# Two attention layers with feed-forwards: adding the turned maxima to the queries on TensorE and ScalarE instead of VectorE

## The reference, cut to what matters

```python
f = log_sigmoid(x @ Wf.T + bf)              # per head
c = cumsum(f, axis=1)
scores = einsum('bihd,bjhd->bhij', q, k) / sqrt(8)
scores = scores + (c[:, :, None, :] - c[:, None, :, :]).transpose(0, 3, 1, 2)
scores = where(tril, scores, -inf)
p = softmax(scores, axis=-1)
o = einsum('bhij,bjhd->bihd', p, v)
```

## Time and profile before

| | before |
|---|---|
| median of 3 runs | 1479.36 us (1478.53 to 1481.83) |
| the profiled execution, its own time | 1476.44 us |
| span of its instructions | 1474.2 us |
| busy over the span: PE, DVE, ACT, POOL | 75%, 78%, 62%, 31% |
| loop of the second attention | about 815 to 1267 us of the span |
| granted TensorE clock, mean of the span | 0.812 |

### The profile page before, as it was taken

The page is one execution under the profiler, slowest core; times in us unless marked ns, Lnnn a source line. Parts: engine busy times, 40 slices in busy tenths (PEclk is TensorE's granted clock), DMA queues, the critical chain, the costliest instruction groups (busy, mean ns, idle before and its releaser), DMA issues. The chain is left out here.

```text
span 1474.2 us, 26809 instructions
## 1 busy us (share of the span) xinstructions
PE 1103.8 (75%) x7861; PEld 517.4 (35%) x7861; DVE 1143.3 (78%) x3615; ACT 910.5 (62%) x1823; POOL 460.4 (31%) x680
## 2 busy tenths in 40 slices
PE   1556666666542799995377899999999999677995
PEld 0112222222232466663254233233233332243654
DVE  4699999999988544443867899999999998377664
ACT  1699999999962244332464566666666666356453
POOL 0132333233220677775102122222222222122331
PEclk9755555555555899998598799999999999799998
DMA  1356867786638222222626111111111111400001
GB/s 57 96 124 139 152 129 139 140 147 133 117 68 235 65 80 76 78 80 96 216 97 191 59 57 53 66 54 56 63 54 59 56 54 37 115 1 1 1 15 44
DMA packets 221078, 128.95 MB, mean 87 GB/s; under 512 B 164632, under 2 KB 200600, under 8 KB 220552
## 3 DMA queue, kind: packets, MB, share of 16 engines
q1 hardware_dynamic: 200312, 100.90, 28.0%
q0 software_dynamic: 6896, 16.04, 3.4%
q10 hardware_dynamic: 13728, 10.30, 2.6%
HBM read 55.60 MB, written 37.62 MB: 63 GB/s over the span
## 5 line engine op out<-in xcount | busy, mean ns | idle before, releaser
L1863 ACT ACTIVATE qkv_made<-qkv_lower 128x1024 f32<-128x1024 f32 (+3 forms) x256 | 208.0, 872 | 105.8 <-PE qkv_lower L1679 105.8
L522 PE MATMUL a_sc<-a_k,a_q 16*128 16x512 bf16 (+3 forms) x384 | 165.4, 504 | 124.2 <-DVE a_mx L701 117.9
L1643 PE MATMUL qkv_upper<-l_k,all_y 64*128 64x512 bf16 (+3 forms) x768 | 211.8, 338 | 44.8 <-DVE qkv_mx L2057 25.3
L2053 DVE CUSTOM_DVE_ANT_0 all_y<-qkv_upper,all_mask 128x384 bf16<-128x384 f32 (+3 forms) x512 | 231.5, 485 | 9.2 <-PE qkv_upper L1643 3.0
L1909 POOL TENSOR_SCALAR_AFFINE_SELECT qkv_made<-qkv_made 128x256 f32<-128x256 f32 x256 | 102.5, 406 | 364.8 <-ACT qkv_made L1863 274.9
L701 DVE CUSTOM_DVE_ANT_0 a_rows<-a_sc,all_mask 128x1024 bf16<-128x1024 f32 (+7 forms) x256 | 191.4, 748 | 8.0 <-PE a_sc L522 7.4
L571 ACT ACTIVATE a_rows<-a_rows 128x1024 bf16<-128x1024 bf16 (+7 forms) x256 | 171.5, 670 | 24.5 <-DVE a_rows L711 24.5
L1679 PE MATMUL qkv_lower<-all_y,l_k 64*128 64x384 bf16 (+3 forms) x768 | 173.5, 330 | 6.6 <-DVE all_y L2074 0.9
L2057 DVE TENSOR_REDUCE qkv_mx<-qkv_upper 128x1 f32<-128x512 f32 x256 | 173.1, 687 | 6.8 <-PE qkv_upper L1643 6.8
L1698 PE MATMUL qkv_upper<-qkv_made,qkv_v_heads 128*32 128x384 f32 (+3 forms) x1920 | 177.5, 433 | 0.0
L580 ACT ACTIVATE a_unread<-a_rows 128x1024 bf16<-128x1024 bf16 (+7 forms) x256 | 171.1, 668 | 0.0
(11 more groups left out here) (258 smaller groups left out, 1897.1 us busy)
## 6 DMA issues: line engine op xcount, KB each, us to landing
qkv_made<-out_rows SPq DMA_DIRECT2D x16, 512.0 KB, 8.0
o_rows<-qkv_made SPq DMA_DIRECT2D x32, 256.0 KB, 2.0
l_k<-k_rows SPq DMA_DIRECT2D x60, 128.0 KB
all_y<-q_rows SPq DMA_DIRECT2D x128, 48.0 KB
a_raw<-in_gate ACTq DMA_DIRECT2D x16, 224.0 KB, 3.2
a_raw<-in_up ACTq DMA_DIRECT2D x16, 224.0 KB, 4.1
ride_wd<-in_down SPq DMA_DIRECT2D x1, 3584.0 KB, 16.9
k_rows<-qkv_parts SPq DMA_DIRECT2D x8, 384.0 KB, 3.3
```

The source lines that it names most:

```text
L522: last = nc.tensor.matmul(sc[:, n % 3, lo // 512, 0:w], q_sb[32 * h:32 * h + hd, u % 2, qb * P:(qb + 1) * P], k_sb[32 * h:32 * h + hd, u % ...
L1643: nc.tensor.matmul(row[:, n % SLOTS, 0:w], q_sb[of_head, u % RING, POS[qb] * P:(POS[qb] + 1) * P], k_sb[of_head, u % RING, lo:lo + w], sta ...
L1863: nc.scalar.activation(probs[:, n % GR, lo:hi], st[:, n % 2, lo:hi], ACT.Exp).then_inc(exp_done, 1)
L2053: nc.vector.tensor_tensor_reduce(out=passed[:, n % SLOTS, 0:w], in0=tile[:, 0:w], in1=mask[:, at:at + w], scale=1.0, scalar=-3e38, op0=ALU ...
```

## The change

The turn becomes two entries, a first and a second half. For each half TensorE writes 512 float32 columns (one slot of `row`): a matmul of the identity with the unit's queries, which puts the queries there, and on top of it, accumulating, the four transposes of the blocks of maxima. ScalarE copies the slot to `q_sb` in bfloat16. VectorE's addition is gone. The halves stand between two pieces in slots 7 and 8, and the pieces behind them are spread so that each of the 12 slots has two pieces. The slots of PSUM held by halves are freed by a new semaphore `turn_copied`, those held by pieces by `row_free`, whose count now leaves the halves out. ScalarE copies the halves of unit u + 1 after the exponentials of groups 8 and 9 of unit u, and those of unit 0 ahead of its first exponentials. The list of semaphores of the expert stage is taken in another order.

```diff
-TURN = "turn"
+TURNS = ("turn first half", "turn second half")
...
 LATER = ((12, 13), (14, 15), (16, 17), (18, 19), (20, 21), (22, 23),
-         (0, 1), (2, 3), (TURN,), (4, 5, 6), (7, 8, 9), (10, 11))
+         (0, 1), (2, TURNS[0], 3), (4, TURNS[1], 5), (6, 7), (8, 9), (10, 11))
...
+            def slot_free(n):
+
+                if n >= SLOTS:
+                    before = entries[n - SLOTS]
+                    if before in turn_of:
+                        pe.wait_ge(turn_copied, turn_of[before] + 1)
+                    else:
+                        pe.wait_ge(row_free, maxed_of[before] + 1)
...
-                if n >= SLOTS:
-                    pe.wait_ge(row_free, n - SLOTS + 1)
+                slot_free(n)
...
-            def turn_max(u):
-
-                n = entry_of[u, TURN]
+            def turn_max(u, what):
+
+                half, n = TURNS.index(what), entry_of[u, what]
                 pe.wait_ge(m_parts, 3 * (u + 1))
-                pe.wait_ge(row_free, n - SLOTS + 1)
-                turned = row[:, n % SLOTS].bitcast(BF16)
-                for qb in range(TB):
-                    last = nc.tensor.transpose(turned[:, POS[qb] * P:(POS[qb] + 1) * P],
-                                               mcol[:, u % 2, qb].rearrange("p h r -> p (h r)"), ident_b[:])
+                slot_free(n)
+                tile = row[:, n % SLOTS]
+                nc.tensor.matmul(tile[:], ident_b[:], q_sb[:, u % RING, 512 * half:512 * (half + 1)], start=True, stop=False,
+                                 skip_group_check=True)
+                for to in range(4):
+                    last = nc.tensor.matmul(tile[:, to * P:(to + 1) * P],
+                                            mcol[:, u % 2, ORDER[4 * half + to]].rearrange("p h r -> p (h r)"), ident_b[:],
+                                            start=False, stop=True, skip_group_check=True)
                 last.then_inc(row_ready, 1)
...
                     if g == 0:
 
-                        pe.wait_ge(row_free, entry_of[u, TURN] + 1)
+                        pe.wait_ge(turn_copied, 2 * (u + 1))
...
             for u, what in opening[NC // 2:]:
                 entry(u, what)
-                if what == TURN:
+                if what == TURNS[1]:
                     pe.wait_ge(remains, len(todo))
...
+            def copy_turned(u, half):
+
+                e = (u, TURNS[half])
+                act.wait_ge(row_ready, entry_of[e] + 1)
+                nc.scalar.copy(q_sb[:, u % RING, 512 * half:512 * (half + 1)], row[:, entry_of[e] % SLOTS]
+                               ).then_inc(turn_copied, 1)
+
+            copy_turned(0, 0)
+            copy_turned(0, 1)
             for u in range(units):
...
                     if g == 0 and u:
                         copy_out(u - 1)
+                    if g in (8, 9) and u + 1 < units:
+                        copy_turned(u + 1, g - 8)
             copy_out(units - 1)
...
-            def add_max(u):
-                n = entry_of[u, TURN]
-                dve.wait_ge(row_ready, n + 1)
-                nc.vector.tensor_tensor(out=q_sb[:, u % RING], in0=row[:, n % SLOTS].bitcast(BF16),
-                                        in1=q_sb[:, u % RING], op=ALU.add).then_inc(row_free, 1)
```

More of the change, by code:

```diff
@@ L409, with of_next @@
 LATER = ((12, 13), (14, 15), (16, 17), (18, 19), (20, 21), (22, 23),
-         (0, 1), (2, 3), (TURN,), (4, 5, 6), (7, 8, 9), (10, 11))
+         (0, 1), (2, TURNS[0], 3), (4, TURNS[1], 5), (6, 7), (8, 9), (10, 11))
+def of_next(what):
+    return what in TURNS or what >= NC // 2
 def row_entries(units):
@@ L420, in row_entries @@
             for what in slot:
-                to = u + 1 if what == TURN or what >= NC // 2 else u + 2
+                to = u + 1 if of_next(what) else u + 2
                 if to < units:
@@ L1071, in experts @@
         at, pos, cnt = ht[:, 0], dn[:, 0], dn[:, 1]
+        scattered = [c.sem(f"scattered{j}") for j in range(OUT)]
         listing = ("tables", "chain", "ex_ready", "ones_set", "ranked", "marked",
@@ L1080, in experts @@
          made_ready) = (c.sem(n) for n in names)
-        scattered = [c.sem(f"scattered{j}") for j in range(OUT)]
         block = ctx.enter_context(nc.Block())
@@ L1416, in project_and_attend @@
     entry_of = {e: i for i, e in enumerate(entries)}
+    turn_of = {e: i for i, e in enumerate(e for e in entries if e[1] in TURNS)}
+    maxed_of = {e: i for i, e in enumerate(e for e in entries if e[1] not in TURNS)}
     with ExitStack() as ctx:
@@ L1460, in project_and_attend @@
         of_y, of_x = Spread(nc, c, "y"), Spread(nc, c, "x")
[L1461 to L1464, removed]
+        turns = ("row_ready", "row_free", "turn_copied", "m_parts", "m_clear", "st_ready", "exp_done",
+                 "masked", "pv_done", "v_ready", "o_copied", "v_clear")
+        (row_ready, row_free, turn_copied, m_parts, m_clear, st_ready, exp_done, masked, pv_done, v_ready,
+         o_copied, v_clear) = (c.sem(n) for n in turns)
         out_stored = [c.sem("out_a"), c.sem("out_b")]
@@ L1711, in _ @@
                 entry(u, what)
-            opening = [(0 if what == TURN or what >= NC // 2 else 1, what) for slot in LATER for what in slot]
+            opening = [(0 if of_next(what) else 1, what) for slot in LATER for what in slot]
             for u, what in opening[NC // 2:]:
                 entry(u, what)
-                if what == TURN:
+                if what == TURNS[1]:
                     pe.wait_ge(remains, len(todo))
@@ L2048, in max_of @@
                 dve.wait_ge(row_ready, n + 1)
-                if n >= SLOTS:
-                    dve.wait_ge(row_free, n - SLOTS + 1)
+                if n >= SLOTS and entries[n - SLOTS] in maxed_of:
+                    dve.wait_ge(row_free, maxed_of[entries[n - SLOTS]] + 1)
                 if lo + w == (qb + 1) * P:
```

9 lines of the change are left out of this document (4 added, 5 removed).

## The result

The changed kernel takes 1494.65 us (median of 4 runs, 1494.09 to 1495.46), the kernel before beside it 1478.94 (4 runs, 1477.57 to 1481.83). The ratio is 1.0104, 95% interval 1.0087 to 1.0122: slower by 15.7 us. The forecast was 1494, slower with a chance of 0.66. The profiled execution took 1494.14 us with a span of 1492.3, 17.7 and 18.1 us more than that of before.

A forecast was written before the change was run, and what follows sets the result against it. A chain of waits between VectorE and TensorE through three PSUM slots bounds the kernel, not VectorE's load. 13.5 us of laps plus 0.5 and 0.5 for the ends make 14.5, giving 1494 us, range 1487 to 1503.

The forecast's parts named there:

- likeliest case: The forecast itself, slower at 1494 us, with its own range of 1487 to 1503 and a chance of 0.60.
- the chain: Second attention: VectorE frees a PSUM slot, TensorE writes the piece ahead of `values`, does `values`, then writes VectorE's next piece.
- the table of steps: Forecast and measured times of nine steps in one lap, from piece 3 written (13.60, 13.66) to group 3's scores (20.75, 20.81).
- The first link: From piece 0 to piece 8 in a lap: piece 8 comes 0.30 us later although VectorE has 0.61 less to do.
- the walk: The forecast's step-by-step path through one lap of the kernel before, with piece 0 at 1012.69 and the 1000 left out.
- The second link: From piece 8 to 15: group 3's scores wait for group 1's exponential, so piece 15 comes 0.15 us more late.
- The laps: A lap, one unit's period in the second attention (14.05 us), grows by 0.45; 30 full laps give 13.5 us.
- The ends: First turn, between 0.6 gained and 1.3 lost, taken as 0.5 us lost; last lap, without pieces, 0.5 us.
- ScalarE at no cost: Two copies a lap, 1.16 us, fit ScalarE's 4.59 us of idle; they cost nothing as work but count as a link.
- VectorE is the bound: Rival, faster: time falls with VectorE's work, by 19 us to 1460 or 38 us to 1441; chance 0.26.
- The tie: Rival: the delay of piece 3 and the copy is 0.45 us smaller, 0.1 a lap either way, 1476 to 1482; chance 0.08.
- The clock: Rival: TensorE's granted clock falls to 1.2 GHz at times, a half costs 0.45 us more, 1520 us; chance 0.06.

The follow-up runs named there:

- e11: The changed kernel with the two copies of the halves taken by VectorE instead of ScalarE: 1541.67 us, 1.0139 of the kernel before, lap 14.69 us.
- e4: The kernel before with the turn between pieces 4 and 5 and piece 6 alone in slot 9: 1507.10 us, 0.9942 of the kernel before, lap 13.68.
- e3: The changed kernel with each half's identity matmul issued twice: 1509.20 us, 1.0218 of the kernel before, lap 15.02 us.
- e5: The changed kernel with both halves in slot 8, pieces 5, 6 in slot 9, 7 to 9 in slot 10, copies after group 9: 1523.29 us, ratio 1.0039.
- e6: The changed kernel with one more ScalarE copy between the second half's arrival and its copy: 1511.72 us, 1.0227 of the kernel before, lap 15.10.
- e13: The changed kernel with the two waits ahead of each half swapped, the slot's first: 1540.34 us, 1.0121 of the kernel before, lap 14.51.
- e10: The changed kernel with ScalarE's copy of a unit's result moved behind group 1's exponential: 1532.66 us, 1.0085 of the kernel before, lap 14.45.
- e7: The changed kernel with one more ScalarE copy after group 7's exponentials, where ScalarE is idle: 1496.24 us, 1.0128 of the kernel before, lap 14.59.

## Why the prediction was right

**The result.** 1494.65 for 1494, slower, within the likeliest case's own 1487 to 1503. That it is this close is in part luck. The sum was 14.5 us in terms of the profiled execution, and that one grew by 17.7 (1476.44 to 1494.14): the sum is 3.2 us short. The medians differ by 15.7 only, since the profiled execution of the kernel before lay 2.5 us below its median and that of the changed kernel 0.5. The direction and the chain are not luck, as the table of steps shows.

**What bounds the kernel.** The forecast said: not VectorE's load but a chain through TensorE's list and three slots. e11 (1.12 us more of VectorE's work for 0.11 us of lap), e4 (the same work, 0.37 less) and e3 (0.44 of TensorE's work for 0.44 of lap, though by the profile TensorE is idle for 1.4 us of the changed kernel's lap: 14.58 - 12.95, less the 0.22 of the missing record) show it from three sides. (The 6 us without streaming in the expectation of e3 stand in no row.) TensorE's work alone isn't the bound either: e5 has the changed kernel's work in a lap 0.44 shorter, and e6's 0.52 came from ScalarE.

**The first link, 0.30, measured 0.37.** Piece 8 stands at 18.12 on the walk's scale for 17.75. The walk had the first half wait "exactly as piece 3 did". It doesn't: piece 3 had one wait and the half has two, and the one that ends last became an instruction of its own. That is the missing 0.07 (e13). The old turn had such an instruction too (line 1650 in the trace of before). The other terms hold: a half of 0.55 (from 1023.27 to 1023.81 it is 0.54), the copy's 0.58, the 1.20 from piece 7 to the next unit's group 0 (1024.56 to 1025.76).

**The second link, 0.15.** Behind piece 15 stand the `values` of slot 1. In TensorE's timeline of the kernel before:

```profile
1006.79 1.06 PE L1698 MATMUL qkv_upper<-qkv_made,qkv_v_heads 128*32 128x512 f32 x8
```

One lap on, that is 1006.79 + 14.05 = 1020.84. In the changed kernel they start at 1029.44, which is 1021.37 on the walk's scale. That is 0.53 later, 0.16 more than the first link's 0.37. e10 gave back 0.13.

**The laps.** 0.45 forecast, 0.53 to 0.54 measured. 30 laps of the missing 0.08 are 2.4 us, most of the 3.2 us by which the sum is short.

**The ends.** 0.5 and 0.5 forecast. The first lap grew by about 0.6 us, 0.1 over the others, with 0.4 ahead of it; 1.0 came behind the last. No run was made for the ends; their parts were not told apart.

**ScalarE at no cost.** Right as work (e7: nothing), right as a link (e6: 0.52 for a copy more).

**The rivals.** "VectorE is the bound" falls with e11. The tie asked for 0.45 less of delay in the waits; none was there. The clock stayed at 1.00 in every lap read.

**A size that was off.** VectorE's busy time was forecast at 12.3 a lap and is 12.51, probably since records that used to overlap at their edges (0.69 us long, 0.61 from start to start) now stand apart; its idle time, over 2 us, is 2.07.

## What to carry to other kernels

Where engines hand work to each other through a few slots, follow one period of the order of waits before relieving the busiest engine: an engine busy 92% of the time had, with its work cut, only more to wait for. Ask of each long block in an in-order list which item stands just ahead of it and what that item waits for; moving one such piece behind the block gave 0.7% with no instruction changed. Moving work to an idle engine gave nothing, since it cost the engine between the two, TensorE, half a microsecond more a lap. Of two waits ahead of one instruction, the one that comes last belongs where the instruction itself carries it; in both orders tried here that was the one written first.

## What the runs showed of the hardware that was not expected

A wait as an instruction of its own (its record is 51 ns long) costs about 0.07 us over one carried by the weight load when it is the one that ends last (e13: 0.64 to 0.58 in the wait, 14.58 to 14.51 in the lap), and the profile then names the wrong releaser, since the load carries the semaphore that was done earlier (at 1020.87, for a load at 1021.17).

A copy of 128x512 from float32 to bfloat16 by VectorE out of PSUM takes 0.69 us (e11; 0.61 from start to start), by ScalarE 0.585 (changed kernel): at this size ScalarE is not the slower one.
